# Second cross attention of a two-layer decoder on one core: the weighting of the output by the softmax share, the sum over heads and the last key's values arranged anew

## The reference, cut to what matters

```python
def _L1_xattn_ref(x, context, Wq, Wk, Wv, Wo, bo):
    q = (x @ Wq.T).reshape(b, t, h, s)
    k_ = (context @ Wk.T).reshape(b, tc, h, s)
    v = (context @ Wv.T).reshape(b, tc, h, s)
    inv4 = e ** (-0.25)
    dot = jnp.einsum('bthd,bchd->bhtc', q * inv4, k_ * inv4)
    attn = jax.nn.softmax(dot, axis=-1)
    out = jnp.einsum('bhtc,bchd->bthd', attn, v).reshape(b, t, e)
    return out @ Wo.T + bo
...
x = x + _L1_xattn_ref(_layernorm(x, axis=-1), ctx_1024, L1_xattn_Wq, ...)
```

## Time and profile before

| | |
|---|---|
| median of three runs | 1639.16 us (1632.37 to 1641.44) |
| the profiled execution, its own time | 1640.08 us |
| its span | 1638.1 us |
| granted TensorE clock, mean | 0.88 of full speed |
| busy: PE / DVE / ACT / POOL, share of the span | 78% / 67% / 51% / 47% |
| first to last maximum of the pass (L1633) | 645.4 to 1203.5 us, 256 instructions |

### The profile page before, as it was taken

How to read it: one execution, slowest core, us unless ns; L and a number is a source line. 1 busy time by engine, 2 the same in 40 slices (tenths; PEclk the granted TensorE clock), 3 DMA queues, 4 the chain that set the end, 5 groups by cost and what they waited for, 6 DMA issues and landing times. The chain is left out here.

```text
span 1638.1 us, 48674 instructions
## 1 busy us (share of the span) xinstructions
PE 1280.6 (78%) x15138; PEld 1107.7 (68%) x15139; DVE 1093.9 (67%) x3599; ACT 840.1 (51%) x2658; POOL 771.2 (47%) x1508
## 2 busy tenths in 40 slices
PE   3878789897659995888888888888869898529991
PEld 2656778786659994666666666666648787529991
DVE  4555377877356663888888888888868977523334
ACT  1554256564224442666666666666646756315440
POOL 2555033767546653444443444444333465646661
PEclk9898588888579997999999999999978989659996
DMA  7997552221122212121111111111000000022225
GB/s 224 254 251 196 207 166 69 60 60 50 36 63 67 63 53 89 60 66 67 32 32 48 32 32 44 36 32 32 27 14 2 10 22 25 32 61 72 68 59 164
DMA packets 91996, 122.00 MB, mean 74 GB/s; under 512 B 12689, under 2 KB 67218, under 8 KB 91858
## 3 DMA queue, kind: packets, MB, share of 16 engines
q1 hardware_dynamic: 74194, 82.77, 17.3%
q0 software_dynamic: 12288, 34.82, 7.3%
q10 hardware_dynamic: 5376, 2.63, 0.5%
HBM read 89.68 MB, written 30.49 MB: 73 GB/s over the span
## 5 line engine op out<-in xcount | busy, mean ns | idle before, releaser
L1586 ACT ACTIVATE p_prob<-six,p_nm 128x257 f32<-128x257 f32 x512 | 235.9, 474 | 187.4 <-DVE p_nm L1633 180.5
L1720 POOL TENSOR_TENSOR p_spread<-p_both,sb_const 128x256 f32<-128x256 f32 x128 | 78.4, 613 | 248.1 <-DVE p_both L1674 190.5
L1633 DVE TENSOR_REDUCE p_nm<-six 128x2 f32<-128x514 f32 x256 | 164.7, 684 | 10.2 <-PE six L1493 4.8
L1493 PE MATMUL six<-p_kv,p_q_all 32*128 32x257 f32 x1024 | 92.2, 426 | 94.7 <-ACT p_prob L1586 94.5
L1823 PE MATMUL bank<-sb_w,m_experts_aT 128*128 x1152 | 155.7, 278 | 6.9 <-ACT m_experts_aT L1852 4.4
L1839 PE MATMUL six<-m_experts_xT,m_experts_w 128*128 128x128 f32 x1152 | 156.0, 279 | 0.1
L1802 POOL DMA_INDIRECT expert_outputs<-m_experts_y,m_experts_dest x144 | 142.6, 990 | 26.1 <-POOL m_experts_tiny L1801 14.7
L1823 PEld LDWEIGHTS bank<-sb_w,m_experts_aT 128*128 128x128 f32 x1152 | 140.4, 192 | 11.9 <-issue 11.7
L776 POOL DMA_INDIRECT expert_inputs<-p_r_x,p_r_slot x128 | 126.2, 986 | 41.6 <-issue 34.0
L1839 PEld LDWEIGHTS six<-m_experts_xT,m_experts_w 128*128 128x128 f32 x1152 | 143.3, 196 | 0.7 <-issue 0.3
L1514 PE MATMUL six<-sb_const,p_prob 128*128 128x128 f32 x1024 | 138.1, 280 | 1.8 <-ACT p_pT L1602 1.6
(11 more groups left out here) (282 smaller groups left out, 3404.4 us busy)
## 6 DMA issues: line engine op xcount, KB each, us to landing
ctxN_ring<-ctxN POOLq DMA_DIRECT2D x32, 516.0 KB, 11.3
ctxT_ring<-ctxT SPq DMA_DIRECT2D x32, 514.0 KB, 12.0
p_ctxT<-ctxT SPq DMA_DIRECT2D x32, 514.0 KB, 3.6
m_experts_x<-expert_inputs SPq DMA_DIRECT2D x144, 64.5 KB
bd_scores<-p_rows SPq DMA_DIRECT2D x32, 256.0 KB, 2.8
p_bd<-bd_scores SPq DMA_DIRECT2D x32, 256.0 KB
sb_w<-w SPq DMA_DIRECT2D x32, 256.0 KB
p_y<-expert_outputs SPq DMA_DIRECT2D x32, 128.0 KB, 3.5
```

Source lines behind the costliest of these rows:

```text
L1493: last = mm(scores_ps[:, g, 0:CTX], q_all[rows, t.par, b], kT[rows, t.par, b, :], start=True, stop=True, tile_position=(32 * g, 0))
L1586: last = nc.scalar.activation(prob[:, b, g, :], scores_ps[:, g, 0:CTX], ACT.Exp, bias=nm[:, b % 2, g:g + 1], accum_out=total[:, b % 2, g:g ...
L1633: nc.vector.tensor_reduce(nm[:, b % 2, g:g + 2], scores_ps[:, g:g + 2, 0:CTX], AX.X, ALU.max, negate=True).then_inc(s[most], 1)
L1720: nc.gpsimd.tensor_tensor(spread[:, u % 2], both[:, u % 2].rearrange("p k g -> p (k g)").unsqueeze(2).unsqueeze(3).broadcast_to([P, 2 * G, ...
```

## The change

The computation stays the same, arranged as share times o_ps summed over heads, plus the last key's part brought in by a second product with Wo. Part by part:

1. DVE's `finish` becomes two instructions a sequence: a copy of `share_ps` to SBUF, and `masked` = o_ps times that copy, written head by head into a buffer that holds a whole tile. L1614, L1617 and L1625 go.
2. In step 0 the two stand ahead of `normed` instead of behind it.
3. The sum over four heads is made once a tile by GpSimd, at the head of its step 2: `halves` (128x256) and `oT` (128x128), one waiting for the other.
4. The last key's values are multiplied once a tile, by DVE in step 2 (`end_v`, 128x128), and added by a second product with Wo that accumulates in PSUM. PE waits for `end_v` in step 2 before it writes `end_ps` again.
5. The second transpose of `shares` becomes a product with a constant 0/1 matrix of 32 columns (C_R4) that also sums over heads; its output is 32 columns of `end_ps` for each sequence, so that a tile fills 128.
6. DVE's copy of the last key's exponentials (L1673) goes; GpSimd's one product of 128x256 becomes two of 128x128, the second waiting for the first.

The diff, without the lists of semaphores and with less context:

```diff
@@ -1439,9 +1440,10 @@
...
         nm, total = (sb(n, [P, 2, G]) for n in ("nm", "total"))
-        both = sb("both", [P, 2, 2, G])
-        spread = sb("spread", [P, 2, 2 * G, H4, HD])
-        ended, whole, shared = (sb(n, [P, P]) for n in ("ended", "whole", "shared"))
+        recip = sb("recip", [P, 2, G])
+        spread = sb("spread", [P, 2, 2, G, H4, HD])
+        share, masked, halves = sb("share", [P, 2, P]), sb("masked", [P, 2, H4, P]), sb("halves", [P, 2, P])
+        end_v = sb("end_v", [P, 2, P])
         y = sb("y", [P, 2, TOPK * D])
...
@@ -1519,18 +1521,21 @@
...
                 if t.live:
-                    pe.wait_ge(s["shared"], seq(t, u))
+                    pe.wait_ge(s["masked"], seq(t, u))
                 if b == 1 and at(2).live:
...
                     pe.wait_ge(s["q"], at(2).nth())
+                if b == 2 and at(4).live:
+                    pe.wait_ge(s["end_v"], at(4).nth())
                 if b == 3 and at(4).live:
...
                 pe.wait_ge(s["spread"], seq(t, b))
-                for out, first in ((share_ps, 0), (end_ps, G)):
-                    nc.tensor.transpose(out, spread[:, b % 2, first:first + G].rearrange("p g h d -> p (g h d)"), ident)
+                nc.tensor.transpose(share_ps, spread[:, b % 2, 0].rearrange("p g h d -> p (g h d)"), ident)
+                mm(end_ps[:, b * LEN:(b + 1) * LEN], spread[:, b % 2, 1].rearrange("p g h d -> p (g h d)"),
+                   c[:, C_R4:C_R4 + LEN], start=True, stop=True)
 
...
@@ -1563,8 +1568,9 @@
...
                     if b == 2 and prev.live:
-                        pe.wait_ge(s["oT"], seq(prev, B4 - 1))
-                        mm(misc_ps, oT[:, prev.par, :], m.w["WoT_x"][:, :], start=True, stop=True).then_inc(s["y_ps"], 1)
+                        pe.wait_ge(s["oT"], prev.nth())
+                        mm(misc_ps, oT[:, prev.par, :], m.w["WoT_x"][:, :], start=True, stop=False)
+                        mm(misc_ps, end_v[:, prev.par, :], m.w["WoT_x"][:, :], start=False, stop=True).then_inc(s["y_ps"], 1)
                     if t.live:
...
@@ -1576,7 +1582,7 @@
...
                         if past(cur, b, 4):
-                            act.wait_ge(s["ends"], seq(cur, b, 4))
+                            act.wait_ge(s["spread"], seq(cur, b, 4))
                             act.wait_ge(s["pT_ps"], seq(cur, b, 4))
...
@@ -1606,24 +1612,19 @@
...
 
+            def take_share(t, b):
+                dve.wait_ge(s["o_ps"], seq(t, b))
+                if past(t, b, 2):
+                    dve.wait_ge(s["masked"], seq(t, b, 2))
+                nc.vector.tensor_copy(share[:, b % 2, :], share_ps).then_inc(s["share"], 1)
+
             def finish(t, b):
-                dve.wait_ge(s["o_ps"], seq(t, b))
-                n = t.n * B4 + b
-                if past(t, b, 1):
-                    dve.wait_ge(s["whole"], seq(t, b, 1))
-                nc.vector.tensor_scalar(ended[:, :], end_ps, m.last_values[:, n:n + 1] if t.known else
-                                        m.last_values[:, DS(n, 1)], None, ALU.mult).then_inc(s["ended"], 1)
-                dve.wait_ge(s["ended"], seq(t, b))
-                nc.vector.tensor_tensor(whole[:, :], o_ps, ended[:, :], ALU.add).then_inc(s["whole"], 1)
-                dve.wait_ge(s["whole"], seq(t, b))
-                if past(t, b, 1):
-                    dve.wait_ge(s["oT"], seq(t, b, 1))
-                nc.vector.tensor_tensor(shared[:, :], whole[:, :], share_ps, ALU.mult).then_inc(s["shared"], 1)
-                dve.wait_ge(s["shared"], seq(t, b))
-                if b == 0 and t.past(2):
-                    dve.wait_ge(s["y_ps"], t.before(2))
-                nc.vector.tensor_reduce(oT[:, t.par, b * LEN:(b + 1) * LEN],
-                                        shared[:, :].rearrange("p (h i) -> p i h", h=H4), AX.X, ALU.add).then_inc(s["oT"], 1)
+                dve.wait_ge(s["share"], seq(t, b))
+                if t.past(2):
+                    dve.wait_ge(s["halves"], t.before(2))
+                nc.vector.tensor_tensor(masked[:, t.par, :, b * LEN:(b + 1) * LEN], o_ps.rearrange("p (h i) -> p h i", h=H4),
+                                        share[:, b % 2, :].rearrange("p (h i) -> p h i", h=H4),
+                                        ALU.mult).then_inc(s["masked"], 1)
 
...
@@ -1636,14 +1637,22 @@
...
                 for b in range(B4):
+                    t, u = near(at, b, -3)
+                    if t.live:
+                        take_share(t, u)
+                        finish(t, u)
+                    if b == 2 and prev.live:
+                        if prev.past(2):
+                            dve.wait_ge(s["y_ps"], prev.before(2))
+                        nc.vector.tensor_tensor(
+                            end_v[:, prev.par, :].rearrange("p (b i) -> p b i", b=B4), end_ps.rearrange("p (b i) -> p b i", b=B4),
+                            m.last_values[:, prev.cols(B4)].unsqueeze(2).broadcast_to([P, B4, LEN]),
+                            ALU.mult).then_inc(s["end_v"], 1)
                     if b == 0 and nxt.live:
...
                         normed(m, z[:, nxt.par, :], nxt, m.RZ).then_inc(s["z"], 1)
-                    t, u = near(at, b, -3)
-                    if t.live:
-                        finish(t, u)
                     if b == 1 and nxt.live:
...
@@ -1669,9 +1678,8 @@
...
                         if past(t, u, 2):
-                            dve.wait_ge(s["spread"], seq(t, u, 2))
-                        nc.vector.tensor_copy(both[:, u % 2, 1, :], prob[:, u, :, LAST]).then_inc(s["ends"], 1)
-                        nc.vector.reciprocal(both[:, u % 2, 0, :], total[:, u % 2, :]).then_inc(s["recip"], 1)
+                            dve.wait_ge(s["spread_share"], seq(t, u, 2))
+                        nc.vector.reciprocal(recip[:, u % 2, :], total[:, u % 2, :]).then_inc(s["recip"], 1)
                         dve.wait_ge(s["pT_ps"], seq(t, u))
...
@@ -1684,7 +1692,7 @@
...
         def _(pool):
-            mine = c[:, C_M4P:C_M4P + H4].unsqueeze(1).unsqueeze(3).broadcast_to([P, 2 * G, H4, HD])
+            mine = c[:, C_M4P:C_M4P + H4].unsqueeze(1).unsqueeze(3).broadcast_to([P, G, H4, HD])
 
...
@@ -1696,6 +1704,14 @@
...
                                                 ALU.mult).then_inc(s["k_end"], 1)
+                    if b == 2 and prev.live:
+                        pool.wait_ge(s["masked"], seq(prev, B4 - 1))
+                        nc.gpsimd.tensor_tensor(halves[:, :, :], masked[:, prev.par, 0:2, :], masked[:, prev.par, 2:4, :],
+                                                ALU.add).then_inc(s["halves"], 1)
+                        pool.wait_ge(s["halves"], prev.nth())
+                        if prev.past(2):
+                            pool.wait_ge(s["y_ps"], prev.before(2))
+                        nc.gpsimd.tensor_tensor(oT[:, prev.par, :], halves[:, 0, :], halves[:, 1, :], ALU.add).then_inc(s["oT"], 1)
                     done, u = near(at, b, -1)
...
@@ -1714,12 +1730,15 @@
...
                         pool.wait_ge(s["recip"], seq(done, u))
-                        pool.wait_ge(s["ends"], seq(done, u))
                         if past(done, u, 2):
                             pool.wait_ge(s["o_ps"], seq(done, u, 2))
-                        nc.gpsimd.tensor_tensor(spread[:, u % 2],
-                                                both[:, u % 2].rearrange("p k g -> p (k g)").unsqueeze(2).unsqueeze(3).broadcast_to(
-                                                    [P, 2 * G, H4, HD]), mine, ALU.mult).then_inc(s["spread"], 1)
+                        nc.gpsimd.tensor_tensor(spread[:, u % 2, 0],
+                                                recip[:, u % 2, :].unsqueeze(2).unsqueeze(3).broadcast_to([P, G, H4, HD]),
+                                                mine, ALU.mult).then_inc(s["spread_share"], 1)
+                        pool.wait_ge(s["spread_share"], seq(done, u))
+                        nc.gpsimd.tensor_tensor(spread[:, u % 2, 1], spread[:, u % 2, 0],
+                                                prob[:, u, :, LAST].unsqueeze(2).unsqueeze(3).broadcast_to([P, G, H4, HD]),
+                                                ALU.mult).then_inc(s["spread"], 1)
                     if b == 2 and at(1).live:
...
```

More of the change, by code:

```diff
@@ L1419, in cross_many_heads @@
         "z", "zT_ps", "zT", "q_ps", "q", "kv_ps", "kv", "k_end", "scores", "most_a", "most_b", "exp_b", "pT_ps",
-        "pT_a", "pT_b", "recip", "ends", "spread", "o_ps", "ended", "whole", "shared", "oT", "y_ps", "xb", "weighted")}
+        "pT_a", "pT_b", "recip", "spread_share", "spread", "o_ps", "share", "masked", "end_v",
+        "halves", "oT", "y_ps", "xb", "weighted")}
     ctx_in = [m.sem("p6_ctx_in_a"), m.sem("p6_ctx_in_b")]
```

## The result

The kernel after takes 1579.96 us (median of four runs, 1572.29 to 1585.83), the kernel before beside it 1636.33: a ratio of 0.966, 95% interval 0.963 to 0.969. That is 56 us less where 39.7 were forecast, and outside the range of 1592 to 1618. The profiled execution has a span of 1576.9 us, 61.2 less than before.

The account below looks back on a forecast made before the run. A ring of scores, maxima and exponentials was taken as the bound; 0.80 and 0.60 saved less 0.12 made 1.28 us a tile, 31 times 39.7 us, from 1639.16 to about 1600 us, range 1592 to 1618.

Parts of the forecast that it names:

- step 0: First of a tile's four steps, 5.37 us with the loop's branch, 4.84 without; forecast to get 0.80 shorter.
- step 2: Third of a tile's four steps, 5.05 us, its maxima behind `finish` and the queries' layout; forecast to get 0.60 shorter.
- The ring: Scores, maxima, exponentials and next scores wait on one another in turn; a sequence takes as long as one turn.
- steps 3: Last of a tile's four steps, 3.67 us, the ring's shortest turn with DVE ready in time; no gain forecast.
- steps 1: Second of a tile's four steps, 3.61 and 3.66 us, filled by PE's own work; forecast to grow by 0.12.
- Saved: 0.80: DVE's row ahead of the maxima in step 0, forecast to shrink from 1.58 to 0.78 us.
- Saved: 0.60: DVE's row ahead of the maxima in step 2, forecast to shrink from 1.92 to 1.32 us.
- about 0.12 to PE: Product of 32 columns replacing a transpose, 0.23 against 0.105 us a sequence; forecast to count in step 1 alone.
- Rival C: The product of 32 columns costs PE nothing more: 3.6 us more gain, 1596 us; chance 0.08.
- `oT` at 2.11: GpSimd's sum over heads in step 2, forecast ready 2.11 us after the scores, with cover of 0.6.
- rival A: GpSimd's split product comes late for step 1 and PE waits for it: 1615 us; chance 0.14.
- Rival E: PE's clock stays at the lower level in some tiles, slower than before: 1654 us at 6 tiles; chance 0.03.

Follow-up runs that it names:

- e12: Kernel before with L1614 always reading column 0 of the last values, a fixed address: a pair of tiles takes 34.70 us, 0.27 less.
- e2: Kernel before with only the order changed, `finish` ahead of z in step 0: a pair of tiles takes 34.84 us, against 34.97.
- e3: Kernel after with the order undone, `finish` behind z again in step 0: a pair of tiles takes 32.15 us, 0.11 more.
- e6: Kernel after with the product of 32 columns made twice: a pair of tiles takes 32.48 us, 0.22 more in each step 1.
- e1: Kernel before with filler on PE, two more products with Wo and three more transposes of z a tile: 1577.01 us against 1588.85.
- e9: Kernel before with filler on PE made of transposes alone, four in step 2 and three in step 0: 1621.36 us against 1630.56.
- e4: Kernel before with L1614 taking the last key's values as a broadcast tensor instead of a pointer scalar: a pair takes 34.72 us.

## Why the prediction was wrong, point by point

- **The ring, and which steps pay.** Right. Steps 0 and 2 shrank, steps 3 stayed at 3.66, steps 1 grew a little. The direction and the mechanism were forecast; the size was not, by two terms: the start of DVE's row, and the clock.
- **Parts 1 and 2, "Saved: 0.80" and "Saved: 0.60".** The intervals between DVE's instructions came out within 0.02 in step 2. In step 0 z follows the product after 0.29 (927.83 − 927.54), not 0.21, and in the tile with the branch it is 0.42 from copy to product and 0.41 to z. What failed is where the row of them starts. The sum took `finish` to begin where it had begun before, 0.25 after the scores of step 2 and, in step 0, where z had stood, 0.40 after them (924.69 − 924.29). The copy begins 0.15 and 0.20 after them. "Moving `finish` ahead of z costs nothing" was so. What makes the copy early in step 2 is that it has no address computed from a register (e12), down to the end of `weigh` in one of the tiles. In step 0 it is also that z, which has three, no longer stands at the head; that part is read from the rows and from e2, not shown by an edit of z. Of the 0.37 a pair that were missed (2.93 against 2 x 1.28), the two steps 2 hold 0.25 (4.36 and 4.35 where 4.51 and 4.45 were forecast, 5.11 and 5.05 less 0.60). Their start came 0.16 and 0.11 earlier, of which e12 gives 0.10 and 0.11. The steps 1 hold 0.07 (3.72 twice instead of 3.73 and 3.78), the steps 0 only 0.03 (4.63 and 3.95 instead of 4.57 and 4.04), as the wider intervals took back most of their earlier start. The order has 0.13 by e2 and 0.11 by e3.
- **Part 5, "about 0.12 to PE".** Right in kind: step 1 grew by 0.11 and 0.06. The next product starts only 0.14 after the one with 32 columns (905.24 to 905.38), but the next weight load 0.23 after its load (905.13 to 905.36, and 0.22 elsewhere), and the 0.22 of e6 is that of the loads. Rival C, by which it would have been free, is out. The figure that it took from the Trainium skill (TensorE: Matmul & The Clock Gate, Back-to-back issue gap) is given there for the gap between products by itself; of a stream of weight loads and products the same section says that both set the spacing. The trace agrees with the latter.
- **Part 4** cost nothing, as said. PE's idle time ahead of the scores of step 3 is still 0.34.
- **Part 3, `oT` at 2.11.** Measured 2.11, and that is luck: `masked` is done after 0.77 instead of 0.85, `halves` takes 0.73 instead of 0.61, and `oT` starts 0.07 after it and not 0.19.
- **Part 6 and rival A.** The price was taken from the wrong rows in both directions: with a broadcast operand 128x128 takes 0.40, not 0.46, and the second starts 0.48 after the first, so the pair takes 0.89 instead of 1.11; `halves` with two full operands takes 0.73, not 0.61. Neither is waited for. Of a lockout between z and GpSimd the rows show little: GpSimd's 128x1 instruction at 912.35, beside z, took 0.26 where its like takes 0.19. Rows of the kernel after, by lines from 700 to 1000 us:

```profile
L1739 POOL TENSOR_TENSOR p_spread<-p_spread,p_prob 128x128 f32<-128x128 f32 x75 | 30.6, 408 | 5.9
L1735 POOL TENSOR_TENSOR p_spread<-p_recip,sb_const 128x128 f32<-128x128 f32 x75 | 30.1, 401 | 38.3 <-DVE p_recip L1682 38.3
...
L1709 POOL TENSOR_TENSOR p_halves<-p_masked 128x256 f32<-128x256 f32 x19 | 13.8, 727 | 24.2 <-DVE p_masked L1625 24.2
```

- **Rival E, the clock.** This is the larger part of the miss. The sum put the clock at nothing: the text read 0.98 in the earlier trace rows as speaking against rival E and argued only for what would follow if the clock fell. But 0.98 of 70 us at levels 1 and 0.5 is 2.8 us at the lower one (3.4 by the finer window), and since step 1 is PE's own work, such a stretch comes through: 1.66 us each, six times, 10 us. "PE will idle less" was said, and its consequence, that the stretches would go, was not priced.
- **The two together.** The steady part was missed by 31 x (1.46 − 1.28) = 6 us, the clock's by 10. Either alone would have left the measured 1579.96 below the range's lower end (1586 and 1582 instead of 1592); with 31 x 1.46 + 10 = 55 the forecast would have been 1584.
- **The range.** Two slips in the working changed nothing: by its own terms step 0's lower bound is 0.80 − 0.12 = 0.68, not 0.66, and 31 x 0.12 is 3.7, not 3.6.
- The experiments on the clock (e1, e9) show that filling PE makes the stretches vanish. Why they come in every second pair of before (and in every third of e4 and e12) stays open; that wasn't tried.

## What to carry to other kernels

A granted clock a little under 1 in a window is not a rounding: find the stretch, see whether PE's work sets the time there, and count it as something that a change can give back, by leaving PE less idle. When instructions are taken from the head of an in-order queue, price also when the new head can start, not only the durations behind it: here an address computed from a register cost 0.1 us there, and a fixed one nothing. And what stands ahead of the instruction that a ring waits for is paid for, by as much as it delays that start (0.46 and 0.22 for z, where its removal was put at 0.68 and 0.27), until the moved piece is itself waited for by another engine, as end_v was.

## What the runs showed of the hardware that had not been expected

- Filler on TensorE, 0.8 us in a tile of 17.5, products or transposes alike, removed all low-clock stretches from the ring's steady part and made the pass 9 us shorter (558.1 to 549.0).
- A product of 32 columns with full 32-bit weights costs 0.22 us where PE is the bound (e6). That is also what lies between the weight loads of two products with 128 columns (905.36 and 905.58 in the kernel after).
- An operand address computed from a register cost DVE 0.1 us at the start of L1614 at the head of its queue: 0.21 behind the norm's aggregate with it, 0.11 with a fixed column (e12). Beside these stand, not varied by themselves, 0.29 for z with three such addresses and 0.10 for the copy where nothing else holds it (902.78 − 902.68).
- The steady pair repeats to 0.01 us on chips on which the whole kernel before differs by 40 us.
